# Attention 1 of a four-stage kernel: query and output products of split operands, outputs a quarter of a batch later, the largest |x3| from each row's ends

## The reference

```python
def _L1_xattn_ref(query, key, value, Wq, bq, ..., Wm, bm):   # query: 8 x 256 x 1024, 16 heads of 16
    q = _conv1x1(query, Wq, bq)                   # 256x256 times 256x1024 a batch
    k = einsum('bdn,nk->bdk', _conv1x1(key, Wk, bk), proj_k)       # 64 projected keys
    v = einsum('bdn,nk->bdk', _conv1x1(value, Wv, bv), proj_v)
    scores = einsum('bdhn,bdhk->bhnk', q, k) / HD ** 0.5
    prob = softmax(scores, axis=-1)
    x = einsum('bhnk,bdhk->bdhn', prob, v)
    return _conv1x1(x.reshape(b, HD * H, -1), Wm, bm)

x = x + tanh(g_xattn[1]) * _L1_xattn_ref(_layernorm(x), ctx, ctx, ...)
x = x + tanh(g_ffn[1]) * _L1_ffn_ref(_layernorm(x), weight)   # its input is scaled by 448 / max|layernorm(x)|
```

## Time and profile before

| | us |
|---|---|
| median of 3 runs (lowest to highest) | 1406.97 (1406.61 to 1411.55) |
| the profiled execution itself | 1410.53 |
| its span | 1408.7 |
| PE busy | 1310.4 (93%) |
| DVE busy | 892.4 (63%) |
| ACT busy | 689.7 (49%) |
| POOL busy | 348.2 (25%) |
| granted PE clock, mean | 0.972 |

### The profile page before, as it was taken

The page is one execution under the profiler, slowest core; times in us unless marked ns, Lnnn a source line. Parts: engine busy times, 40 slices in busy tenths (PEclk is TensorE's granted clock), DMA queues, the critical chain, the costliest instruction groups (busy, mean ns, idle before and its releaser), DMA issues. The chain is left out here.

```text
span 1408.7 us, 25944 instructions
## 1 busy us (share of the span) xinstructions
PE 1310.4 (93%) x9723; PEld 1039.8 (74%) x9731; DVE 892.4 (63%) x1444; ACT 689.7 (49%) x1762; POOL 348.2 (25%) x403
## 2 busy tenths in 40 slices
PE   6999789999999999887999999999969999998498
PEld 5999789989989999855788888888834555454244
DVE  4452468768777786755223346668846587886897
ACT  4222067777767777764111101003326666665396
POOL 0000023122231321111101014224232444443324
PEclk9999899999999999999999999999979999999799
DMA  6752463745646557774563626011335454444123
GB/s 224 243 176 79 123 174 103 204 136 132 173 120 171 127 155 165 165 206 136 174 209 116 228 93 251 30 61 45 97 93 133 112 119 105 104 101 93 60 101 139
DMA packets 138324, 192.79 MB, mean 137 GB/s; under 512 B 31815, under 2 KB 101575, under 8 KB 137312
## 3 DMA queue, kind: packets, MB, share of 16 engines
q1 hardware_dynamic: 138208, 191.16, 47.3%
HBM read 95.92 MB, written 35.29 MB: 93 GB/s over the span
## 5 line engine op out<-in xcount | busy, mean ns | idle before, releaser
L1264 ACT ACTIVATE a_prob<-a_psS,a_negmax 128x256 f32<-128x256 f32 x512 | 238.0, 490 | 91.5 <-DVE a_negmax L1154 90.9
L1154 DVE TENSOR_REDUCE a_negmax<-a_psS 128x4 f32<-128x1024 f32 x128 | 153.6, 1201 | 38.0 <-PE a_psS L1013 38.0
L989 PE MATMUL a_psQ<-a_xT_hi,wide 128*128 128x256 f32 x912 | 176.6, 293 | 0.0
L1491 PE MATMUL m_psY<-wide,m_a_hi 128*128 128x512 f32 x512 | 159.8, 394 | 6.8 <-DVE m_a_lo L1539 6.8
L1491 PE MATMUL m_psY<-w_ffn,m_a_hi 128*128 128x512 f32 x512 | 158.3, 390 | 0.0
L1281 ACT COPY a_probT<-a_psT 128x512 f32<-128x512 f32 x208 | 115.7, 605 | 67.7 <-PE a_psT L1022 67.6
L989 PEld LDWEIGHTS a_psQ<-a_xT_hi,wide 128*128 128x128 f32 x912 | 140.6, 191 | 0.1
L1022 PE MATMUL a_psT<-ident,a_prob 128*128 128x128 f32 x1024 | 135.4, 276 | 0.0
L989 PE MATMUL a_psQ<-a_xT_lo,wide 128*128 128x256 f32 x456 | 128.4, 282 | 0.0
L1022 PEld LDWEIGHTS a_psT<-ident,a_prob 128*128 128x128 f32 x1024 | 117.1, 142 | 0.9 <-issue 0.8
L1491 PEld LDWEIGHTS m_psY<-wide,m_a_hi 128*128 128x128 f32 x512 | 97.1, 190 | 27.6 <-DVE m_a_lo L1539 7.0
(11 more groups left out here) (248 smaller groups left out, 2673.2 us busy)
## 6 DMA issues: line engine op xcount, KB each, us to landing
a_q_stack<-a_q_hi SPq DMA_DIRECT2D x128, 128.0 KB, 3.0
a_q_stack<-a_q_lo SPq DMA_DIRECT2D x128, 128.0 KB, 2.4
b_q_stack<-b_q_hi SPq DMA_DIRECT2D x128, 128.0 KB, 2.4
c_raw<-lay_ctxT SPq DMA_DIRECT2D x16, 512.0 KB, 4.7
rows<-in_x SPq DMA_DIRECT2D x8, 1024.0 KB, 5.3
scratch_o<-rows SPq DMA_DIRECT2D x16, 512.0 KB, 3.3
m_x<-in_x SPq DMA_DIRECT2D x8, 1024.0 KB, 5.7
scratch_x<-m_x SPq DMA_DIRECT2D x8, 1024.0 KB, 5.1
```

What stands on the lines that cost most here:

```text
L989: last = nc.tensor.matmul(bank[:, 0:S], w[:, kt, t * P:(t + 1) * P], a[:, u, kt, :], start=(kt == 0 and w is wq.hi and a is xT_hi), stop=( ...
L1154: nc.vector.tensor_reduce(negmax[:, n % 2, :], psS[:, bank:bank + 2, :].rearrange("p a (j k) -> p (a j) k", k=S), AX_X, ALU.max, negate=Tr ...
L1264: last = nc.scalar.activation(prob[:, n % 2, j, :], psS[:, 2 * (n % 2) + j // 2, (j % 2) * S:(j % 2 + 1) * S], ACT.Exp, bias=negmax[:, n % ...
L1491: last = nc.tensor.matmul(psY[:, 2 * t + h, :], a[:, u, kt, rows_t], m[:, kt, cols], start=(kt == 0 and a is a_hi and m is w.hi), stop=(kt ...
```

## The change

- Queries (all but batch 0) and outputs (all but batch 7) become three rounded products for each plain one: high weight by high input, high weight by low input, low weight by high input. The weights are split once (`high_weight` on ACT, `low_weight` on POOL). xn is split by two rounded copies on ACT and two subtractions on DVE in steps 1 and 3; o by a rounded copy on ACT and a subtraction on POOL, one tile in each step, a step after `normalise_o`.
- The output of tile k of batch b-1 moves from step (b, k) to step (b, k+1); the last one of a batch goes to (b+1, 0), and that of batch 6 into step (7, 3), in place of a query.
- The low halves lie where their float32 sources lie (xn, o, q share memory with xn_lo, o_lo, q_lo), q gets four buffers instead of two, the mask is loaded as 128x8 and read broadcast, and `spread_raw` shares memory with y.
- `x3n` and its maxima are gone: DVE takes the maximum and the minimum of each x3 row (`ends_x3`), and `largest_x3` takes the greater distance from the mean times the reciprocal standard deviation.

```diff
     def output_of(b, k):
-        return (b - 1, *tile_of(k))
+        return (b - 1, *tile_of(k - 1)) if k else (b - 2, *tile_of(TILES - 1))
...
+        def normalised(b, k):
+            return (b - 1 if k < 2 else b, 1 if k < 2 else 0, k % 2)
...
         # POOL
+            def low_o(b, h, t):
+                n = o_index(b, h, t)
+                cols = slice(h * HALF_N, (h + 1) * HALF_N)
+                pool.wait_ge(o_high, n + 1)
+                nc.gpsimd.tensor_tensor(o_lo[:, t, cols], o[:, t, cols], plain(o_hi)[:, t, cols], ALU.subtract
+                                        ).then_inc(o_split, 1)
...
                 if real(b + 1):
                     low_query(b + 1, k)
                 if k == 2 and real(b + 2):
                     block_keys(b + 2)
                 ob, t, h = output_of(b, k)
+                if (b, k) == (-1, TILES - 1):
+                    low_weight(0, wqT)
+                    low_weight(1, wmT)
                 if real(ob):
                     add_output(outputs, ob, t, h)
                     outputs += 1
...
+                if split_o(*step_before(b, k)):
+                    low_o(*normalised(*step_before(b, k)))
...
         # PE
+            def three_parts(bank, w, dt, rows, moving):
+                hi, lo = moving
+                nc.tensor.matmul(bank, w_hi[:, w, dt, rows], hi, start=(dt == 0), stop=False)
+                nc.tensor.matmul(bank, w_hi[:, w, dt, rows], lo, start=False, stop=False)
+                return nc.tensor.matmul(bank, w_lo[:, w, dt, rows], hi, start=False, stop=(dt == CT1 - 1))
...
             def query(a, k, dt):
...
+                elif dt == 0:
+                    pe.wait_ge(weight_split, 1)
+                    pe.wait_ge(xn_split, xn_index(a, h) + 2)
...
             def output(n, b, t, h, dt):
...
-                    pe.wait_ge(q_ready, min(TILES * (b + 2) + 2 * h + t, TILES * B))
+                    pe.wait_ge(q_ready, min(TILES * (b + 2) + 2 * h + t + 1, TILES * B))
...
+                        pe.wait_ge(weight_split, 2)
+                        pe.wait_ge(o_split, 4 * b + 2 * h + 2)
...
         # DVE
+            def low_xn(b, h):
+                cols = slice(h * HALF_N, (h + 1) * HALF_N)
+                for t in range(TT):
+                    dve.wait_ge(xn_high, xn_index(b, h) + t + 1)
+                    nc.vector.tensor_tensor(xn_lo[:, t, cols], xn[:, t, cols], plain(xn_hi)[:, t, cols], ALU.subtract
+                                            ).then_inc(xn_split, 1)
...
+            def ends_x3(b, t):
+                if b:
+                    dve.wait_ge(largest_done, 4 * b)
+                nc.vector.tensor_reduce(ends[:, 0, t:t + 1], x[:, b, t, :], AX_X, ALU.max).then_inc(ends_done, 1)
+                nc.vector.tensor_reduce(ends[:, 1, t:t + 1], x[:, b, t, :], AX_X, ALU.min).then_inc(ends_done, 1)
+            def largest_x3(b):
+                # four operations on 128x2: max - mean, mean - min, the greater, times rstd
...
                 if k == 3 and real(b - 2):
-                    keep_x3(b - 2)
-                    for t in range(TT):
-                        normalise_x3(b - 2, t)
+                    ends_x3(b - 2, 0)
                 if scored:
                     maximum(sa, sk, 2)
                     maximum(sa, sk, 3)
...
+                if k == 1 and b >= 0 and real(b + 1):
+                    low_xn(b + 1, 1)
+                if k == 3 and real(b + 2):
+                    low_xn(b + 2, 0)
                 if k == 3 and real(b - 2):
-                    for t in range(TT):
-                        largest_x3(b - 2, t)
+                    ends_x3(b - 2, 1)
+                    keep_x3(b - 2)
+                    largest_x3(b - 2)
...
         # ACT
                 if real(b):
                     exponential(b, k, 2)
                     exponential(b, k, 3)
+                if split_o(*step_before(b, k)):
+                    high_o(*normalised(*step_before(b, k)))
+                if k == 1 and real(b + 1):
+                    high_xn(b + 1, 1)
+                if k == 3 and real(b + 2):
+                    high_xn(b + 2, 0)
...
                 if k % 2 == 0 and real(sb_):
                     high_reciprocals(sb_, sh_)
                 if k == 1 and real(b + 1):
                     high_keys(b + 1)
```

More of the change, by code:

```diff
@@ L1887, in _ @@
             load_v1(0)
-            for tile, name in ((sum_of, "sum_of"), (spread_raw, "spread")):
-                sp.dma_start(tile[:], c[name]).then_inc(consts_loaded, 16)
+            for tile, name in ((sum_of[:], "sum_of"), (spread_raw, "spread")):
+                sp.dma_start(tile, c[name]).then_inc(consts_loaded, 16)
             sp.dma_start(wmT[:, :, :], c["wm1T"]).then_inc(wm_loaded, 16)
@@ L1971, in query @@
                         pe.wait_ge(q_ready, TILES * a + k)
-                last = nc.tensor.matmul(query_bank(a, k), wqT[:, dt, t * P:(t + 1) * P], xn[:, dt, h * HALF_N:(h + 1) * HALF_N],
-                                        start=(dt == 0), stop=(dt == CT1 - 1))
+                rows, cols = slice(t * P, (t + 1) * P), slice(h * HALF_N, (h + 1) * HALF_N)
+                if a == 0:
+                    last = nc.tensor.matmul(query_bank(a, k), wqT[:, dt, rows], xn[:, dt, cols],
+                                            start=(dt == 0), stop=(dt == CT1 - 1))
+                else:
+                    last = three_parts(query_bank(a, k), 0, dt, rows, (xn_hi[:, dt, cols], xn_lo[:, dt, cols]))
                 if dt == CT1 - 1:
@@ L2067, in output @@
                         pe.wait_ge(o_copied, TILES * B)
[L2068 to L2070 removed]
+                    if n >= TILES * (B - 1):
+                        pe.wait_ge(o_ready, 4 * b + 2 * h + 2)
+                    else:
+                        pe.wait_ge(weight_split, 2)
+                        pe.wait_ge(o_split, 4 * b + 2 * h + 2)
+                bank, rows, cols = output_bank(b, 2 * h + t), slice(t * P, (t + 1) * P), slice(h * HALF_N, (h + 1) * HALF_N)
+                if n >= TILES * (B - 1):
+                    last = nc.tensor.matmul(bank, wmT[:, dt, rows], o[:, dt, cols], start=(dt == 0), stop=(dt == CT1 - 1))
+                else:
+                    last = three_parts(bank, 1, dt, rows, (o_hi[:, dt, cols], o_lo[:, dt, cols]))
                 if dt == CT1 - 1:
@@ L2118, in _ @@
                         query(b + 1, k, dt)
+                    elif (b, k) == LAST:
+                        output(outputs, B - 2, *tile_of(TILES - 1), dt)
+                outputs += (b, k) == LAST
                 if turned:
@@ L2242, in _ @@
                 normalise_o(B - 1, 1, t)
+            for t in range(TT):
+                ends_x3(B - 2, t)
             keep_x3(B - 2)
[L2244 to L2247, removed]
+            largest_x3(B - 2)
             stats_x3(B - 1, TILES * B - 1)
+            ends_x3(B - 1, 0)
             dve.wait_ge(added, TILES * B)
             moments_x3(B - 1)
+            ends_x3(B - 1, 1)
             keep_x3(B - 1)
[L2252 to L2255, removed]
+            largest_x3(B - 1)
         @block.scalar
@@ L2277, in copy_query @@
                     act.wait_ge(scores_full, 4 * (n - TILES + 1))
-                for dst in (q[:, k % 2, :], q_hi[:, k, :]):
+                for dst in (q[:, k, :], q_hi[:, k, :]):
                     last = nc.scalar.activation(dst, query_bank(a, k), ACT.Identity, bias=bq[:, t:t + 1])
@@ L2311, in copy_o, with high_xn, high_o, high_weight @@
                 nc.scalar.copy(o_raw[:, k, :], psO[:, :]).then_inc(o_copied, 1)
+            def high_xn(b, h):
+                cols = slice(h * HALF_N, (h + 1) * HALF_N)
+                for t in range(TT):
+                    act.wait_ge(x2_norm.normed, 4 * b + 2 * h + t + 1)
+                    nc.scalar.copy(xn_hi[:, t, cols], xn[:, t, cols]).then_inc(xn_high, 1)
+            def high_o(b, h, t):
+                cols = slice(h * HALF_N, (h + 1) * HALF_N)
+                act.wait_ge(o_ready, o_index(b, h, t) + 1)
+                nc.scalar.copy(o_hi[:, t, cols], o[:, t, cols]).then_inc(o_high, 1)
+            def high_weight(w, raw):
+                nc.scalar.copy(w_hi[:, w], raw[:, :, :]).then_inc(weight_high, 1)
             act.wait_ge(bm_gated, 1)
```

81 lines of the change are left out of this document (59 added, 22 removed).

## The result

The changed kernel takes 1466.36 us (median; 1463.95 to 1469.05) beside 1409.26 us of the kernel before on the same chip: ratio 1.0405, 95% interval 1.0365 to 1.0444. It is slower, by 57 us, where 1453 was forecast; the measured time lies in the range (1422 to 1473) but just above the likeliest case's own range (1440 to 1466).

The account below looks back on a forecast made before the run. PE was taken to bound the kernel; its savings, five stalls and the clock, over all rounds and the tail, summed to +45.6 us on 1406.97, so 1453 was forecast, range 1422 to 1473, likeliest case 1440 to 1466.

Parts of the forecast that it names:

- What PE saves: Six rounded products replace each output and query product on PE, saving 0.36 and 0.45 us: 3.24 us a round.
- Stall 1: The output in step 3 waits for POOL's low half of o, made last in step 2: 4.35 us a round.
- Stall 2: The output in step 1 waits for POOL's low half of o, without block keys ahead: 1.8 us a round.
- Stall 3: The first S of step 2 waits for ACT's query copy, behind the o and xn copies: 1.7 us a round.
- Stall 4: In the second half of step 2 PE waits for DVE's maxima, behind low keys and low xn: 1.15 us a round.
- The port: DVE's low xn in step 1 might pay 1.0 us beside POOL; five rounds would add 5, 1458 instead of 1453.
- Stall 5: In step 0 PE waits for DVE's maximum, behind low xn and x3's reductions and small operations: 2.3 us a round.
- The clock: PE's clock falls to the lower level behind the longest wait, before step 3's output: 1.5 us a round, bounds 0 and 4.4.
- The clock holds: Rival: PE's clock stays up through the idle gaps, 1445 us; chance 0.2.
- More clock and port: Rival: half speed from output to values, 2.9 us more in five rounds, and 1.0 of port: 1472 us; chance 0.15.
- POOL early enough: Rival: POOL's low half of o causes no waits before outputs; DVE bounds rounds of 33 us, 1408 in all; chance 0.07.
- Faster: Rival: all added work fits in the other engines' slack and PE stays the bound, 1386 us; chance 0.08.

Follow-up runs that it names:

- c_fill: The changed kernel with twelve rounded products, overwritten by the output, put into PE's longest wait, in step 3: 1458.50 us, ratio 1.0348 to the kernel before.
- p: h_relisted with x3's small operations on POOL, first rows' ends moved to step 2 and o normalised ahead of them: 1401.46 us, 0.9948 of the kernel before.
- a_lowo_first: The changed kernel with POOL making the low half of o first in each step instead of last: 1427.88 us, ratio 1.0141 to the kernel before.
- h_relisted: The changed kernel with POOL's and ACT's split work reordered and xn's low halves on POOL instead of DVE: 1410.54 us, 1.0018 of the kernel before.
- b_xn_pool: The changed kernel with xn's low halves made on POOL, first in steps 1 and 3, instead of DVE: 1452.31 us, ratio 1.0302 to the kernel before.

## Why the prediction was right, and where its sizes were off

The direction, the five stalls and what causes each came out as forecast; the change is slower by 57 us where 45.6 were summed. c_fill is the cleanest measure of the terms, since its clock stays up. The idle times in its rows are 3.8, 2.1, 1.5, 0.7 and 1.7 us, but the last four count from the modelled end of a product. From start to start, as the prediction counted, less the undisturbed distance (0.23 behind a P, 0.35 behind the turn, 0.34 behind the P that follows the values), the five stalls are 3.8, 2.3, 1.8, 0.85 and 1.9: 10.6 of the 40.9, and 30.3 are PE's own. The stalls below are counted so.

- **What PE saves.** 3.24 a round were expected and 0.9 of today's small waits were to go, leaving 28.9 of PE's own. It is 30.3 in c_fill and about 30.5 in p. An output takes 1.39, and 1.47 behind a wait (in the change, from 1182.19 to the P at 1183.66); a query takes 1.47 up to the values. Both stood at 1.36, so 2.5 a round are saved and not 3.24: the 0.1 a product that stood as the worst case. The rest are restarts (behind a wait S is followed after 0.34 in place of 0.24) and small waits of the kernel before that did not go.
- **Stall 1**, 4.35 expected: 3.35 in the change, 3.8 in c_fill. The block keys were summed at 2.52 and take 2.05. Its mechanism is shown by a_lowo_first: with the low half first every wait for it is gone.
- **Stall 2**, 1.8: 1.2 in the change, 1.8 in c_fill and in batch 6.
- **Stall 3**, 1.7: 0.85 in both. The copies do stand ahead of the query copy, but back to back they are shorter than the 1.8 taken (1.56 from 1185.49 to 1187.05). Behind the output's end at 1183.66 the query copy is done at 1189.54, 5.9 and not 6.5, and PE is there 0.2 later than counted.
- **Stall 4**, 1.15: 1.9 in both. The low xn was summed at its undisturbed 1.3 and takes 3.36 beside POOL's low query, addition and low half of o, while the low keys, summed at 2.44, now miss POOL and take 1.41: 1.0 more in all. "The port" kept this out of the sum and priced it at 1.0; as a sum that was right, though it had the low keys pay too. The Trainium skill, "SBUF — State Buffer", section "SBUF: two separate sides", where a DVE instruction with two SBUF inputs and a GpSimd instruction block each other for whole instructions, agrees with these rows and with the 128x2 operation that takes 1.23 for 0.15.
- **Stall 5**, 2.3: 2.1 in the change, 2.3 in c_fill. This is partly luck: of DVE's way to the maximum, copies and low xn take 4.3 from the output's end in place of 5.1, and the copies and small operations of x3 2.5 in place of 1.1, since two of them meet POOL (0.89 and 1.23 us).
- **DVE's sum** was to be 30.7 a round and is 33.0: the low xn beside POOL and those small operations.
- **Sum of a round** without the clock, 40.1: c_fill's 40.9 is near, but by two errors that cancel in part, 1.4 too little of PE's own and 0.7 too much of stalls.
- **The clock**, 1.5 a round with bounds of 0 to 4.4: 3.3 in the profiled pair, about 1.5 by the medians. Where it falls was wrong: not only behind stall 1. The queries of step 2, behind stall 4, and those of step 0, behind stall 5, also stand at 0.43 from start to start. The rule that gaps up to 1.87 leave no mark did not hold here.
- **All rounds.** Batches 2 to 5 were to cost 34.2 and cost 42.1: on average 2.6 more in each of the first three (1.8 of clock, 0.8 of the sum above). Batch 5 came out as forecast by luck: its clock was at 0.92 and it hardly has stall 2 (0.22 idle). Batch 6 was to cost 1.9 and cost 5.3, at a full clock: its stalls 1 to 4 are 6.0 for the 6.5 expected, 1.6 more stand in step (7, 0), where none was counted, and PE's own part was again taken 2 us too low. Tail: 3.2 in place of 2.6.
- **The rivals.** "The clock holds" (1445): the change's clock does not hold, and in c_fill, where it does, the time is 1454 in the profiled execution and 1458.5 by the median, 9 to 13 over that price. "More clock and port" (1472) named the two things that the forecast left out. The result lies 6 us under it and 13 over the forecast, though the lower clock falls in other places than this rival said: of the two, the one with the lower chance came nearer. "POOL early enough" (1408) is not what the change does; a_lowo_first builds just that and takes 1428. DVE is the bound there, as this rival said, but with 33 to 34 us of work and not 30.7, so its price was 20 us too low. h_relisted comes near the price (1410.5) only by taking the low xn off DVE too. "Faster" (1386) would need both lists redone and x3's small operations off DVE; what that gives is p's 1401, with 30.5 us a round of PE's own.
- **The signs.** Rounds were to be 40 to 42 us with PE busy under 80%, and are 44.2 with 81%; the waits for POOL's low half of o were to be 4 and 1.5 to 2, and are 3.1 and 0.96 idle; the clock is under 1 in every full round but that of batch 6. The kinds of wait are those that were named.

## What to carry to other kernels

Before adding work to an engine with a fixed list, ask for each new item what must pass ahead of it, and put it at the earliest step at which its input exists: the same work cost 57 us in one order and nothing when the lists were redone and xn's low halves moved to POOL. A split of operands costs PE less and everyone else more, so the saving is real only when DVE's and POOL's lists have been cut for it. Then look for the next wait one product further on: in p a wait of 1.56 us went and one of 0.55 came there.

## What the runs showed of the hardware that I had not expected

- What DVE's instructions lose beside POOL's is large and doesn't go by their size. Two subtractions of 128x512 take 3.36 us in place of 1.29, operations on 128x2 1.15 to 1.25 in place of 0.15, a copy of 128x2 0.89 in place of 0.16; even `normalise_x2`, with one large input, has a mean of 1170 ns in a_lowo_first, where it is 542 in the kernel before. POOL's own go from 1.27 to 1.72. The reductions of the stream (1.2) and what reads PSUM (`normalise_o` 0.68, the maxima 0.67) are the same in all kernels, within 2%. So work that moves to POOL to relieve DVE comes back in part.
- With one gap of PE filled, the other gaps of 1.7 and 2.1 us left the clock at 1.00; in the change, gaps of 1.68 and 1.91 in the same places were followed by the lower level of 1.2 GHz (products 0.43 apart). The length of one gap did not decide it; what does was not tested.
- POOL's block keys take 2.05 us for two with the mask read broadcast from 128x8, and took 2.52 with a full mask; it is 2.50 to 2.52 in both kernels with the full mask, and 2.03 to 2.06 in the others but b_xn_pool (2.23).
